# Two device loops of a Perceiver layer written out in full: seven passes of the cross-attention loop, five steps of the self-attention loop

## What is computed

```
x = x + cross_attention(layernorm(x), ctx)   # 16 heads of 128; ctx has 1601 rows of 128 channels per item
x = x + self_attention(layernorm(x))         # 16 heads of 16; q, k, v rounded to fp8 with one scale each
x = x + gated_attention(layernorm(x))        # each row's key/value head is the gate's top one; causal
```

## Time and profile before

| | |
|---|---|
| median of 3 runs | 1466.46 us (1465.87 to 1466.65) |
| the profiled execution, own time | 1466.3 us |
| its span, first to last instruction | 1464.5 us |
| what lies around the span | 1.8 us |
| mean granted TensorE clock | 0.976 of full speed |
| HBM traffic | 22.44 MB read, 1.05 MB written |
| instructions in the trace | 31654 |
| packets of instructions fetched, queue 14 and queue 8 | 175 and 20 |
| one pair in the main loop (first transpose of pair 6 to that of pair 7) | 136.49 us |
| one step of the self-attention loop (line 1725, psK, to the next) | 15.47 us |

### The profile page before, as it was taken

One profiled execution on the slowest core, in us unless ns is written; L12 is line 12 of the kernel. 1 busy time (PEld: TensorE's weight loads), 2 busy tenths in 40 slices (PEclk: granted clock), 3 DMA queues, 4 the chain that ended last, 5 costly groups with the idle time before them and its releaser, 6 DMA issues. The chain is left out here.

```text
span 1464.5 us, 31654 instructions
## 1 busy us (share of the span) xinstructions
PE 1377.9 (94%) x5980; PEld 934.4 (64%) x5980; DVE 1262.4 (86%) x5010; ACT 1196.8 (82%) x4845; POOL 1059.2 (72%) x1583
## 2 busy tenths in 40 slices
PE   6997999999999999999999999999999998957886
PEld 4774666666666666666666666666666666845554
DVE  6998889898998899898989899998899898766894
ACT  5897898889888988889888889898988887435673
POOL 5886889888988888898889888988888884000000
PEclk9998999999999999999999999999999999977997
DMA  3000000000000000000000000000000001000000
GB/s 138 0 23 24 1 24 2 24 3 24 1 23 2 23 2 23 11 14 22 2 25 0 24 2 24 1 23 2 24 11 17 23 30 65 1 1 1 8 11 12
DMA packets 10211, 25.25 MB, mean 17 GB/s; under 512 B 848, under 2 KB 6640, under 8 KB 9888
## 3 DMA queue, kind: packets, MB, share of 16 engines
q1 hardware_dynamic: 9728, 23.49, 4.4%
q10 hardware_dynamic: 288, 0.00, 0.0%
HBM read 22.44 MB, written 1.05 MB: 16 GB/s over the span
## 5 line engine op out<-in xcount | busy, mean ns | idle before, releaser
L1123 ACT ACTIVATE c_unused<-c_prod 124x128 f32<-124x128 f32 x1664 | 493.0, 298 | 88.2 <-DVE c_prod L1344 81.2
L1657 POOL TENSOR_TENSOR c_acc<-c_acc,c_prob 123x1024 f32<-123x1024 f32 (+1 forms) x192 | 461.9, 2406 | 25.1 <-ACT c_prob L1130 24.5
L1355 DVE CUSTOM_DVE_ANT_0 c_multiplied<-psK,c_c 124x128 f32<-124x128 f32 x1664 | 381.7, 285 | 54.9 <-PE psK L920 54.8
L919 PE MATMUL psK<-wkh,c_cTh 128*124 128x512 f32 x832 | 414.2, 498 | 12.7 <-DVE c_cTl L1383 10.2
L939 PE MATMUL psO<-c_prob,raw 123*128 123x512 f32 (+1 forms) x832 | 392.1, 594 | 0.0
L1344 DVE TENSOR_TENSOR c_prod<-psK,c_c 124x512 f32<-124x512 f32 x416 | 286.2, 688 | 55.7 <-PE psK L920 42.1
L920 PE MATMUL psK<-wkl,c_cTh 128*124 128x512 f32 x832 | 329.4, 396 | 0.0
L1123 ACT ACTIVATION_READ_ACCUMULATOR c_unused<-c_prod 124x1 f32 x1664 | 311.7, 187 | 0.0
L1366 DVE TENSOR_TENSOR c_prob<-psS,c_ss 124x512 f32<-124x512 f32 x416 | 265.9, 681 | 0.5 <-POOL c_ss L1640 0.4
L1130 ACT ACTIVATE c_prob<-c_prob,shift 124x1024 f32<-124x1024 f32 x208 | 236.7, 1138 | 0.0
L919 PEld LDWEIGHTS psK<-wkh,c_cTh 128*124 128x124 f32 x832 | 154.2, 185 | 118.5 <-DVE c_ss L1355 47.8
(11 more groups left out here) (328 smaller groups left out, 2255.9 us busy)
## 6 DMA issues: line engine op xcount, KB each, us to landing
raw<-in_ctx SPq DMA_DIRECT2D x16, 799.5 KB
raw<-in_L_xattn_Wq SPq DMA_DIRECT2D x6, 256.0 KB, 7.7
xs<-in_x SPq DMA_DIRECT2D x4, 256.0 KB, 4.6
big<-in_L_xattn_Wk SPq DMA_DIRECT2D x1, 1024.0 KB, 7.5
c_prod<-in_L_xattn_Wo SPq DMA_DIRECT2D x1, 1024.0 KB, 5.2
out<-s_y SPq DMA_DIRECT2D x8, 128.0 KB, 1.7
big<-in_L_ffn_W_qkv SPq DMA_DIRECT2D x1, 768.0 KB, 11.3
raw<-in_L_xattn_Wv SPq DMA_DIRECT2D x1, 768.0 KB, 4.2
```

What stands on the lines that cost most here:

```text
L919: nc.tensor.matmul(psK[0:ROWS, c % 2, :], cTh[:, slot, :], T.wkh[:, cols], start=True, stop=False)
L1123: last = nc.scalar.activation(unused[:, j, :], prod[:, k % 2, c // 2, j * CD:(j + 1) * CD], ACT.Copy, accum_out=ss[:, k % 2, 0, h:h + 1])
L1355: last = nc.vector.tensor_tensor_reduce(multiplied[:, j, :], psK[0:ROWS, 1, cols], c2[:, k % NT, :], 1.0, 0.0, ALU.mult, ALU.add, ss[:, k ...
L1657: nc.gpsimd.tensor_tensor(acc[0:rows, batch % 2, :], acc[0:rows, batch % 2, :], prob[0:rows, probs(s), :], ALU.add).then_inc(S.acc, 1)
```

## The change

In both `pipeline` functions the device loop becomes a loop of the program that writes the kernel, so that its body stands in each engine's instruction stream seven and five times. `i` is then a plain number in every step.

```
@@ cross_attention, pipeline @@
-            with eng.Fori(0, NPAIR - 1) as i:
+            for i in range(NPAIR - 1):
                 for v in steps(i, False):
                     emit(i, *v)
             for v in steps(NPAIR - 1, True):
@@ self_attentions, pipeline @@
             step(0, None, None, None)
             step(1, 0, None, None)
             step(2, 1, 0, None)
-            with eng.Fori(0, NPAIR - 3) as i:
+            for i in range(NPAIR - 3):
                 step(i + 3, i + 2, i + 1, i)
             step(None, NPAIR - 1, NPAIR - 2, NPAIR - 3)
```

## The result

| | before | both loops written out |
|---|---|---|
| median of the runs | 1466.16 us (1465.02 to 1466.65, 4 runs) | 1453.26 us (1449.23 to 1454.14, 4 runs) |
| ratio, 95% interval | | 0.9911 [0.9898, 0.9923] |
| span of the profiled execution | 1464.5 us | 1447.5 us |
| instructions in the trace | 31654 | 29923 |

The change makes the kernel faster by 12.9 us.

A forecast was written before the change was run, and what follows sets the result against it. With no engine having much slack, the pace of successive tile steps was taken as the bound. Gains of 7.4 + 0.06 + 0.6 = 8.1 us off 1466.3 gave 1458.2, stated as 1458.4 us for the median; range 1455.0 to 1462.0.

The forecast's parts named there:

- The jumps: Main loop, step 13: six jumps back lengthen the step, four by 1.31 us and two by 1.09; gain 7.4 us.
- The cluster of fetches at the jump: Sign to look for: queue 14 brings about as many blocks as now, with no cluster of six.
- Entry and exit: Main loop's ends: entry step 0.06 us longer than pair 7's, exit free; gain 0.06 us, bounds 0 to 0.1.
- The body of the main loop: Register operations in the main loop's steps are hidden; gain nothing, bounds -1 to +1 us over 182 steps.
- New fetches for PE: Main loop: PE's code fetched anew each pass, about 25 more blocks on queue 8 and a few; cost 0.
- The fourth rival: Main loop: each of 25 added blocks leaves PE dry like a jump, 31 us less 8.1, giving 1489; 3%.
- The self-attention loop: Its jumps cost nothing; exposed register operations cost 0.10 us in each of five steps; gain 0.6 us, bounds 0 and 1.5.
- The clock in the tail: PE's half-clock stretches after 1303 us may shift: some 6 us gained or about 2 lost; nothing added.
- no-change: Third rival: step at the jump is long for another reason, such as its own work; 1466 us, 3%.
- slower case: Main loop: PE's stream fed from memory throughout, each added block leaving it dry; 1489 us, 3%.
- the one in which the hole comes back in part: Second rival, main loop: one block border per pass costs half a jump, 3.6 us back; 1462.0 us, 4%.
- The first one, the clock: First rival: same mechanism but the tail's clock in another phase; 1452.4 to 1455.8 or 1460.5 us, 13%.

The follow-up runs named there:

- e2_self_only: Only the self-attention loop written out, main loop still a device loop, against the kernel before; 1465.41 us over ten runs, ratio 1.0003.
- e9_pool_signal: Both loops written out plus one more POOL signal between the wait of each running sum (line 1657) and the sum; 1453.07 us, ratio 0.9912.
- e1_main_only: Only the main loop written out, self-attention loop still a device loop, against the kernel before; 1452.46 us, ratio 0.9921.

## Why the prediction was wrong

**The jumps: right.** 7.4 us were forecast, 7.5 measured. The comparison of the same step in a looped and in a written-out pair carried this exactly. The cluster of fetches at the jump is gone too: from 323 to 331 us queue 14 brings nothing.

**Entry and exit: right,** 5.07 against 5.15 us at pair 0, 0.08 us for the 0.06 forecast.

**The body of the main loop: this step failed.** The forecast took it at nothing, with bounds of -1 to +1 us. It gave 6.0 us (steps 0, 11 and 24). The comparison behind it was not the one that was claimed: "the other steps of pairs 6 and 7, the heavier ones too, agree as well". Pair 7 leaves the loop only at step 13. Its steps 0 to 12 are looped like those of pair 6, so of course they agree. In the written-out part, steps 13 to 25, one step does not agree: 24 takes 5.49 us in pair 6 and 5.09 in pair 7, where POOL has no 1559 any more (the next item's work is gone) and 1542 takes 0.69 us instead of 1.24. That step is thus no twin either, but it showed the collision. The two costly places, steps 0 and 11, had no written-out twin in the trace at all, and the honest bound would have been wider. Step 11 stood out in the trace, at 5.78 us against 5.1 for most, and DVE's 1.50 us for an operation that takes 0.69 elsewhere was there to be seen.

What the runs show in place of the zero: in steps 11 and 24, 3.7 us, a later POOL that meets DVE's line 1542. The curve with doses shows that lateness of POOL is enough for it. In step 11 about two thirds of the lateness is a hole of 0.25 us in POOL's stream that goes with the place of the code, and what is left, 0.1 us, may be register operations; no run took these away from POOL alone, and the split was not worked out for step 24. In step 0, 2.3 us: DVE's product comes 0.36 us earlier by the position of the code and 0.08 with the register operation gone; the step as a whole is 0.32 us shorter. So the forecast asked the wrong question of the body, whether register operations cost time. Most of what it left out in steps 0 and 11 lies in where the looped code happened to stand. POOL's hole stood in the list of waits of before, as 1.8 us in 7 places.

**New fetches for PE: right.** 28 blocks more on queue 8 for the 25 and a few, at no visible cost: the steps of 5.07 us kept their length. The fourth rival's mechanism did not come. It is real all the same, as the body of two passes shows: there PE is left dry by a jump, at 6 us a time. In straight code it is not, which the forecast had from its five blocks.

**The self-attention loop: right,** 0.12 to 0.13 us a step for 0.10, which the total can't show (e2_self_only).

**The clock in the tail: open in its phase, as said, and the spread is seen.** In the profiled run of after, the last group of eight at line 1852 ran at full clock, as the chain of waits has it (start, us, what):

```profile
1427.72 2.73 PE psK L1852 x8
...
1434.28 1.13 PE psK L1691 x16
```

against 5.32 and 2.02 us in the earlier trace rows: 3.5 us. The windows view has the clock at full around that group, where the earlier trace rows has it at half:

```profile
1428.50:1435.30 6.80, 4.90 (x62) 3.10 (x60) 2.71 (x6) 2.00 (x7) 0.00 (x0) 1.00 0.00 0
```

This execution took 1449.2 us, the other three 1453.2 to 1454.1. The same code of the tail fell the other way in the profiled run of e9_pool_signal, which took 1454.1 us: 5.32 and 2.02 us for these two groups, and 259.8 us from the last transpose to the end against 254.5 here. So the tail's clock makes a spread of about 4 to 5 us within one kernel; the ten runs of e2_self_only lie from 1460.3 to 1466.9 us. The forecast had expected less of a gamble from three runs within 0.8 us.

**The rivals.** The no-change and the slower case are refuted by the measurement, and with the steps of 5.07 us the one in which the hole comes back in part. The first one, the clock, would have given a time like the measured one, but for a wrong reason: e1_main_only and the table of steps show that the surplus sits in the main loop.

## What to carry to other kernels

Before a looped stretch is compared with a written-out one, mark for each step which kind of code it ran from; what has no twin gets wide bounds. A device loop costs its jump, and the jump's price depends on what the body leaves in each engine's instruction store: here 1.25 us with PE's body held and 6 us without, so half-way unrolling gained nothing (1467.35 us against 1464.5) where full unrolling gained 12.9 us. Two copies of the same body need not run alike, so look for small idle times that stand at one place of the code in every pass: POOL's 0.25 us stood under "issue", DVE's 0.36 us was hidden in a longer wait for PE. Where a DVE operation on SBUF alone takes longer than its siblings, look for POOL beside it: moving one POOL operation by a step gave 7.9 us in the looped kernel, and 0.6 us a pair in the written-out one (its median fell by 6.8 us, more than the steps explain).

## What was not expected of the hardware

A jump in a body of two passes stopped PE for 3.02 us, and behind it PE's granted clock stood at 1.2 GHz for 6.7 us; the jump cost 5.9 to 6.2 us in all. More delay on POOL made the pairs shorter: with eight signals ahead of line 1551 a pair takes 134.2 us, with four 134.6, with none 134.3. And the place of the code alone was worth 0.3 us in step 0 of each pair on DVE, and 0.25 us in step 7 on POOL.
